# One load of all edge data in the head of a graph layer, in place of loads inside its loop

## The reference

```python
C = 0.5 * (cos(edge_length * (PI / 10)) + 1.0) * ((edge_length <= 10) & (edge_length >= 0))
h = gelu(edge_attr @ f_w0 + f_b0)          # 20000 x 50 -> 128
h = gelu(h @ f_w1 + f_b1)
h = gelu(h @ f_w2 + f_b2)
h = gelu(h @ f_w3 + f_b3)
msg = (x @ lin1_w)[src] * (h * C[:, None])
agg = segment_sum(msg, dst, num_segments=1250)     # dst is sorted
out = gelu(agg @ lin2_w + lin2_b) @ lin_w + lin_b
return layernorm(x + out)
```

## Time and profile before

| what | value |
|---|---|
| median of three runs | 312.98 us (311.64 to 314.6) |
| profiled execution | 311.7 us, its span 309.9 us |
| PE matmul busy | 249.1 us, 80% |
| PE weight loads | 161.5 us, 52% |
| POOL busy | 156.9 us, 51% |
| ACT busy | 113.4 us, 37% |
| DVE busy | 103.4 us, 33% |
| mean granted clock of PE | 0.775 of 2.4 GHz |
| DMA | 14,483 packets, 17.54 MB |

### The profile page before, as it was taken

The page is one execution under the profiler, slowest core; times in us unless marked ns, Lnnn a source line. Parts: engine busy times, 40 slices in busy tenths (PEclk is TensorE's granted clock), DMA queues, the critical chain, the costliest instruction groups (busy, mean ns, idle before and its releaser), DMA issues.

```text
span 309.9 us, 3660 instructions
## 1 busy us (share of the span) xinstructions
PE 249.1 (80%) x990; PEld 161.5 (52%) x990; DVE 103.4 (33%) x218; ACT 113.4 (37%) x181; POOL 156.9 (51%) x168
## 2 busy tenths in 40 slices
PE   3697939966995997699399869939984994998990
PEld 3344625735663473566257456625743662665760
DVE  5612430514154051414324141432414052335015
ACT  2544412433353243335224433522442352355033
POOL 7671747374555737455473755546474645630000
PEclk9899985796598579659957965995696599569768
DMA  6530211122112212211221221121122202210002
GB/s 206 154 103 20 68 53 52 27 78 59 42 40 65 68 26 77 60 43 32 66 65 26 77 67 44 34 64 57 34 77 54 57 21 73 64 31 0 0 0 83
DMA packets 14483, 17.54 MB, mean 57 GB/s; under 512 B 6512, under 2 KB 11533, under 8 KB 14478
## 3 DMA queue, kind: packets, MB, share of 16 engines
q0 software_dynamic: 5120, 10.50, 12.9%
q1 hardware_dynamic: 8632, 6.39, 7.2%
q10 hardware_dynamic: 726, 0.59, 0.7%
HBM read 16.19 MB, written 1.28 MB: 56 GB/s over the span
## 4 chain that ended last, share of the span: by engine, by line
PE 67%; another core or an unknown queue 15%; issue 7%; DVE 6%; DMA 2%; DVEq 1%; ACT 1%; SPq 0%; ACTq 0%
PE ps_even L430 9%; PE ps_even L406 9%; PE ps_agg_even L443 8%; PE ps_even L421 8%; PE ps_odd L421 8%; PE ps_agg_odd L443 7%; PE ps_odd L430 7%; PE ps_even L416 3%; PE ps_odd L416 3%; DVE messages L606 2%; DMA tables<-in_edge_tables 2%; DVE pre L591 1%; PE ps_even L507 1%; PE ps_odd L497 1%
## 5 line engine op out<-in xcount | busy, mean ns | idle before, releaser
L272 POOL DMA_INDIRECT gathered<-xf_dram,src_idx x152 | 146.9, 967 | 113.8 <-DVE messages L606 65.6
L443 PE MATMUL ps_agg_even<-onehot,messages 125*128 125x64 f32 x160 | 29.4, 346 | 41.4 <-DVE messages L606 33.9
L319 ACT ACTIVATE h<-ps_even,biases_sb 128x500 f32<-128x500 f32 x61 | 41.1, 674 | 57.7 <-PE ps_even L421 36.4
L443 PEld LDWEIGHTS ps_agg_even<-onehot,messages 125*128 125x128 f32 x160 | 28.1, 259 | 52.8 <-issue 44.1
L319 ACT ACTIVATE h<-ps_odd,biases_sb 128x500 f32<-128x500 f32 x61 | 41.1, 674 | 37.0 <-PE ps_odd L421 26.6
L317 ACT ACTIVATE h<-pre 125x512 f32<-125x512 f32 x40 | 25.2, 630 | 74.3 <-DVE pre L591 56.5
L591 DVE TENSOR_TENSOR pre<-ps_even,row_b_sb 125x512 f32<-125x512 f32 x20 | 13.8, 692 | 86.7 <-issue 55.9
L430 PEld LDWEIGHTS ps_even<-w_mlp_sb,h 128*125 128x125 f32 x160 | 26.4, 249 | 21.3 <-issue 19.1
L443 PEld LDWEIGHTS ps_agg_odd<-onehot,messages 125*128 125x128 f32 x160 | 29.8, 263 | 13.1 <-issue 13.1
L406 PE MATMUL ps_odd<-edge_in,w_mlp_sb 50*128 50x500 f32 x42 | 31.8, 848 | 0.0
L406 PE MATMUL ps_even<-edge_in,w_mlp_sb 50*128 50x500 f32 x42 | 31.6, 841 | 0.2 <-issue 0.2
(11 more groups left out here) (99 smaller groups left out, 159.1 us busy)
## 6 DMA issues: line engine op xcount, KB each, us to landing
edge_in<-in_edge_attrT SPq DMA_DIRECT2D x42, 97.7 KB
gathered<-xf_dram,src_idx POOLq DMA_INDIRECT x152
xf_dram<-xf_sb SPq DMA_DIRECT2D x2, 256.0 KB
lin_xT_sb<-in_lin_xT SPq DMA_DIRECT2D x1, 369.0 KB
src_idx<-in_srcT SPq DMA_DIRECT2D x22, 4.0 KB
lin_xT_sb<-in_lin_xT SPq DMA_DIRECT2D x1, 320.0 KB, 3.5
w_mlp_sb<-in_w_mlp ACTq DMA_DIRECT2D x1, 256.0 KB
out<-normed SPq DMA_DIRECT2D x1, 256.0 KB
```

The costliest lines, as they stand in the source:

```text
L272: nc.gpsimd.indirect_dma_start(out=gathered[:, b, t, :], out_offset=None, in_=xf_dram[:, :], in_offset=bass.IndirectOffsetOnAxis(ap=src_id ...
L319: nc.scalar.activation(out_ap, in_ap, GELU, bias=biases_sb[:, layer:layer + 1]).then_inc(done, 1)
L443: last = nc.tensor.matmul(ps_agg[b][:, 0:WINDOW], messages[:, slot, t, :], onehot[:, p % 2, b * TILES_PER_GROUP + t, :], start=(t == 0), s ...
```

## The change

All edge attributes and all gather indices are brought into SBUF before the loop. edge_in grows from two pairs to all twenty (40,000 bytes a partition), src_idx from 2 x 8 to 160 columns. The input array is laid out anew: one row for each of 114 partitions (50 for the even groups, 14 of zeros, 50 for the odd ones), so that one DMA loads both groups of one or several pairs. Six such DMAs cover the pairs 0, 1, 2-3, 4-7, 8-13 and 14-19; the first two are issued by SP behind the tables, the other four by ACT behind the weights. One DMA of 80 KB brings the indices. SP has nothing to do in the loop. PE's and POOL's pairs 2 to 19 are written out in place of the nine turns; ACT and DVE keep their loops.

```diff
+EDGE_CUTS = ((0, 1), (1, 2), (2, 4), (4, 8), (8, 14), (14, PAIRS))
-        src_idx = sb("src_idx", [ROWS, 2, PAIR_TILES], int32)
-        edge_in = sb("edge_in", [ODD_BASE + EDGE_FEAT, 2, GROUP])
+        src_idx = sb("src_idx", [ROWS, TILES], int32)
+        edge_in = sb("edge_in", [ODD_BASE + EDGE_FEAT, PAIRS, GROUP])
@@ block.sync
-            load_src(0, 0)
+            def load_edges(k):
+                p0, p1 = EDGE_CUTS[k]
+                sp.dma_start(edge_in[:, p0:p1, :], edge_attrT[:, p0:p1, :]).then_inc(edge_loaded[k], 16)
+            sp.dma_start(src_idx[:, :], srcT).then_inc(src_loaded, 16)
             ...
-            load_edges(0, 0)
-            load_src(1, 1)
+            load_edges(0)
+            load_edges(1)
             ...
-            with sp.Fori(0, passes) as r:
-                ...
-            sp.sem_inc(loads_drained, 1)
@@ block.gpsimd
-                with pool.Fori(0, TURNS - 1) as j:
-                    ...
+                for g in range(RAW_GROUPS, GROUPS):
+                    b = g % GATHER_SLOTS
+                    pool.wait_ge(message_done, r * GROUPS + g + 1)
+                    pool.sem_inc(group_begun, 1)
+                    for t in range(TILES_PER_GROUP):
+                        tile = g * TILES_PER_GROUP + t
+                        nc.gpsimd.indirect_dma_start(
+                            out=gathered[:, b, t, :], out_offset=None, in_=xf_dram[:, :],
+                            in_offset=bass.IndirectOffsetOnAxis(ap=src_idx[:, tile:tile + 1], axis=0),
+                        ).then_inc(gather_landed[b], 16)
@@ block.scalar, behind the loads of w_mlp, biases and row_b3
+            for k in range(2, len(EDGE_CUTS)):
+                p0, p1 = EDGE_CUTS[k]
+                act.dma_start(edge_in[:, p0:p1, :], edge_attrT[:, p0:p1, :]).then_inc(edge_loaded[k], 16)
@@ block.tensor
-                with pe.Fori(0, TURNS - 1) as j:
-                    before = r * TURNS + j
-                    for p in (2, 3):
-                        ...
+                for p in range(2, PAIRS):
+                    layer2(first, p)
+                    scatter(first, p - 1, 0)
+                    layer3(first, p, 0)
+                    scatter(first, p - 1, 1)
+                    layer3(first, p, 1)
+                    for k in range(3, len(EDGE_CUTS)):
+                        if EDGE_CUTS[k][0] == p + 1:
+                            pe.wait_ge(edge_loaded[k], 16)
+                    layer1((p + 1) % PAIRS)
+                    layer4(first, p)
```

More of the change, by code:

```diff
@@ L135, in gnn_layer @@
         tables_loaded = sem("tables_loaded")
-        src_loaded = [sem(f"src_loaded_{q}") for q in range(2)]
+        src_loaded = sem("src_loaded")
         w_loaded = sem("w_loaded")
         late_loaded = sem("late_loaded")
-        edge_loaded = [sem(f"edge_loaded_{s}") for s in range(2)]
-        loads_drained = sem("loads_drained")
+        edge_loaded = [sem(f"edge_loaded_{k}") for k in range(len(EDGE_CUTS))]
         raw_landed = [sem(f"raw_landed_{g}") for g in range(RAW_GROUPS)]
@@ L265, in _ @@
                         out=raw_x[:, g, t, :], out_offset=None, in_=x_nodes[:, :],
-                        in_offset=bass.IndirectOffsetOnAxis(ap=src_idx[:, 0, tile:tile + 1], axis=0),
+                        in_offset=bass.IndirectOffsetOnAxis(ap=src_idx[:, tile:tile + 1], axis=0),
                     ).then_inc(raw_landed[g], 16)
[L269 to L275, removed]
             pool.wait_ge(passes_ready, 1)
@@ L280, in _ @@
             with pool.Fori(0, passes) as r:
-                pool.wait_ge(src_loaded[1], r * (16 * TURNS) + 16)
-                for b in (2, 3):
-                    pool.wait_ge(message_done, r * GROUPS + b + 1)
+                for g in range(RAW_GROUPS, GROUPS):
+                    b = g % GATHER_SLOTS
+                    pool.wait_ge(message_done, r * GROUPS + g + 1)
                     pool.sem_inc(group_begun, 1)
-                    gather(b)
-                with pool.Fori(0, TURNS - 1) as j:
[L287 to L294, removed]
+                    for t in range(TILES_PER_GROUP):
+                        tile = g * TILES_PER_GROUP + t
+                        nc.gpsimd.indirect_dma_start(
+                            out=gathered[:, b, t, :], out_offset=None, in_=xf_dram[:, :],
+                            in_offset=bass.IndirectOffsetOnAxis(ap=src_idx[:, tile:tile + 1], axis=0),
+                        ).then_inc(gather_landed[b], 16)
         @block.scalar
@@ L400, in _, with layer1 @@
             pe.wait_ge(w_loaded, 48)
-            def layer1(loads, slot):
-                pe.wait_ge(edge_loaded[slot], loads)
+            def layer1(pair):
                 for b in range(2):
                     rows = slice(b * ODD_BASE, b * ODD_BASE + EDGE_FEAT)
-                    nc.tensor.matmul(ps1[b][:, 0:GROUP], w0[b], edge_in[rows, slot, :],
+                    nc.tensor.matmul(ps1[b][:, 0:GROUP], w0[b], edge_in[rows, pair, :],
                                      start=True, stop=True).then_inc(l1_done, 1)
-            layer1(32, 0)
+            pe.wait_ge(edge_loaded[0], 16)
+            layer1(0)
             pe.wait_ge(passes_ready, 1)
@@ L466, in _ @@
                 layer3(first, 0, 1)
-                next_layer1(first, 0)
+                pe.wait_ge(edge_loaded[1], 16)
+                layer1(1)
                 layer4(first, 0)
@@ L475, in _ @@
                 layer3(first, 1, 1)
-                next_layer1(first, 1)
+                pe.wait_ge(edge_loaded[2], 16)
+                layer1(2)
                 layer4(first, 1)
```

54 lines of the change are left out of this document (5 added, 49 removed).

## The result

The change makes the kernel slower: 339.35 us (median of four, 333.49 to 343.07) against 312.31 (311.58 to 314.6) for the kernel before beside it. The ratio is 1.070, 95% interval [1.058, 1.082]. A slower state of the chip lengthens some executions of every kernel (here two of four, the profiled one of 343.07 us, span 341.2, among them), so ratios, and every "A against B" from here on, are taken between the mean times of the others, here 334.6 against 312.7. These 7% are 22 us. The forecast was 319 with 315 to 326 as its own range: the sign is right, the size is missed by more than a factor of three.

The account below looks back on a forecast made before the run. Hold and clock, not arithmetic or gathers, were taken to set the loop's pace. The late store's 6.4 us plus 0 for the loop, added to the median 312.98, gave 319.4, said as 319; own range 315 to 326, whole range 280 to 328.

Parts of the forecast that it names:

- Loop loads, back edge and written-out code: SP's loop loads, PE's back edge, PE's and POOL's written-out pairs: gain or cost 0, straight code at most 5 us.
- The hold: In head and loop: PE's layer 4 results exist, but the signal freeing their reader, VectorE's bias sum, comes 5 us late.
- The large loads lie on six engines: Head: edge loads of 114 rows use six of 16 DMA engines, 34.5 us of work, full until about 40 us.
- The queues take turns by packet: Head: store packets alternate with ACT's large ones, so the xf_dram stores finish at 36 to 41 us, taken as 38.
- 0 for the loop: Loop's term in the sum: the change neither gains nor costs time there, 0 us.
- The change leaves both alone, so the loop keeps its pace: Loop: gathers and fast short matmuls, taken as the hold's condition, stay, so the pace doesn't change.
- Pairs 2 and 3 need nothing more: Loop start: no further delay after pair 1, as POOL takes 10 us a pair against a pace of 13.7.
- the gathers with fast short matmuls: Head and loop: the hold comes when gathers run while PE does short matmuls at the full clock.
- the 6.4: Head: with gathers begun at 38 us, pair 1's messages come at 49.8 in place of 43.4, 6.4 us later.
- Rival 1: Loop: the hold hangs on SP's loads or the back edge and goes; 258 us, or 288 by half; chance 0.28.
- Rival 2: Head: stores get through early, by byte-wise turns or 16 engines; 313 us, or down to 309; chance 0.20.
- Rival 3: Head: raw_x gathers or PE's code arrive late through six crowded engines; 323 to 333 us; chance 0.10.

Follow-up runs that it names:

- e3: Kernel before with only PE's and POOL's turns written out, SP's loads still in the loop, on a chip without holds: 239.19 us, before 237.47.
- e12: The kernel of e3 on a chip with the holds: 313.21 us, kernel before 311.65.
- e11: The kernel of e6 on a chip with the holds: 313.47 us, kernel before 311.65, ratio 1.011.
- e10: Kernel before without its 152 gathers of xf_dram, messages computed from ones, on a chip with the holds: 209.77 us, against 306.0.
- e4: Kernel before plus ACT's four large loads in the head, into a tile nobody reads, on a chip without holds: 261.47 us, before 237.47.
- e6: Changed kernel, 114 rows, with SP issuing the four large loads after the xf_dram stores landed, on a chip without holds: 238.86 us, before 239.34.
- e9: Changed kernel with 128 rows, large loads behind the stores, eight gather slots for four, VectorE's loop written out, chip with holds: 319.62 us, before 312.3.
- e8: Changed kernel with four spare columns behind each pair, so large loads go in 2,000-byte packets, chip with holds: 334.58 us, before 312.3, ratio 1.084.
- e1: Changed kernel with edge tile and source padded from 114 to 128 rows, on a chip without holds: 245.53 us, before 237.47.

## Why the prediction was wrong

Right were these steps, each with what bears it out. Loop loads, back edge and written-out code are worth nothing that these times show (e3, e12, and e11 with all three gone). The hold needs the gathers: the head of the changed kernel has none while POOL waits, and e10 has none at all; the forecast had this from three places of one trace. The large loads lie on six engines: six of sixteen are 37.5%, and the two queues show 37.9% in 24 to 36 us. The queues take turns by packet. The store is therefore late, pair 1 is late with it, and the order of two issues is the whole loss (e4 makes it on a chip of the second kind; e6 there and e11 on the first kind remove it).

The step that failed is "0 for the loop", with the sentences behind it, "The change leaves both alone, so the loop keeps its pace" and "Pairs 2 and 3 need nothing more: POOL takes 10 us for a pair and the pace is 13.7". It took POOL's idle 113.8 us for slack and the hold for something of a fixed length. But a POOL that starts late finds free slots and runs 24 gathers in a row, and the hold beside them is longer: PE's layer 4 of pair 2 ends at 63.2 us and its sum comes at 77.2, 14.0 us late, where the sums of the kernel before were 4 to 5 late beside bursts of eight. Pair 2's messages are 21.0 us late, and pair 1's second ones had been 10.7. e9 bears this out: its first burst is of 24 gathers too, and VectorE has PE's result of 28.3 us only at 46.1, 17.8 late; beside the 23 of e11 it was 9.6. Why a signal is held longer beside a longer burst isn't shown.

From the first gather to the last it takes 258.6 us before, 254.2 after, and 248 to 262 in e8, e9, e11 and e12, with starts between 14.2 and 43.4. This looks like a phase with a length of its own, so that a later start is paid in full; I don't take it as shown, since pair 1's messages follow the first gather by 6.3 us in the changed kernel and by 27 to 48 in the others. That a store done by 31.6 us would have cost nothing was tested on no chip with the holds. On the other chips the start is paid by a plainer cause, POOL back to back: 192 to 197 us from first to last in e1 to e6.

What pointed at the failed step was in front of me. The earlier trace rows has the held sum at 70.77, and the last gather of its burst, at 68.05 in the same timeline, ends at 69.0. I looked at what starts near the hold (SP's issue, a back edge) and made "the gathers with fast short matmuls" its condition, but never set the hold beside the burst or asked what a longer burst would do to it.

A term of the sum was mis-sized too, the 6.4. The store was priced at 38 us and took until 42.5, and the first messages of pair 1 came when forecast by luck: the 11.8 us from block to messages was read where the gathers had long landed and was used where the gathers themselves were the last to come. The first four give messages 6.3 us after the first gather, the second four 11.3, so the odd group of pair 1 was 10.7 us late. With 6.4 replaced by 10.7 the forecast would have said 324; the other 11 us are about what the lengthened hold adds. A slip without effect on the sum: ACT's rows are of 4,000 bytes too (pairs 2 and 3), and not of 8,000 and 12,000 alone.

Of the forecast's signs the DMA share near 6/16 and pair 1's messages near 50 us came, the latter by that luck. The first gather was due near 38 and came at 43.4. Waits of 4 to 5 us before ps_odd's sum once a turn did not come: the 19 waits of over 2 us on "remote" run from 2.1 to 18.8, eleven of them before other sums.

Rival 1 had the better eye for one thing, that the holds may be worth more than their sum in the chain: where there are none the kernel takes 232 to 244 us, and rival 1 had worked out 258 with a store at 38. But the change doesn't remove their condition. Rival 2's time is what happens with the stores ahead (e6, e11). Rival 3's raw gathers held nobody, but the edges of pair 0 were late, by 5 us in place of 2, hidden in the wait for the store.

Open is what makes the chips differ. The same kernel takes 304 to 322 us on some and 232 to 244 on others, with the holds as the visible difference, and no experiment here could switch them on or off on one chip other than by taking the gathers away. Each chip was used at one time only, so chip and time aren't separated. Which queue or engine keeps PE's signal back while POOL gathers isn't shown either; the profile says only "remote".

## What to carry to other kernels

Before an engine's idle time is taken for slack, set its bursts beside the waits of the others: if the waits lie at its bursts turn after turn, the engine may be part of what sets the pace, however idle it looks, and what a late start does to its bursts has to be priced; a version without its work (e10) tests this. A large load is better issued once the small store that others wait for has landed (here SP issued it then, in place of ACT): the two queues swapped packet for packet on each engine, and 512 bytes then cost as much time as the 12,000 beside them. Loads ahead of the loop didn't pay here, where the loop's loads were hidden: the version without the fault can't be told from the kernel before (1.011 [0.972, 1.050]).

## What the runs showed of the hardware

- One kernel, two paces: 304 to 322 us on two chips and 232 to 244 on two others, in the same code.
- PE's signals reached their readers late while gathers ran, on chips of the first kind: 4 to 5 us beside the bursts of eight of the kernel before, 2 to 7 beside those of the changed kernel, 14.0 beside its burst of 24, 17.8 beside e9's. In the kernel before the wait ended 0.3 to 1.8 us after the burst at ten of ten places. In the changed kernel 12 of 19 such waits end between 0.4 us before and 4.1 after a burst's end; of the others two end 1.1 and 1.2 us before the end of a burst of eight, and five 1.6 to 11.9 us before the end of bursts of 15 or 16. In e11 it is 9 of 19. So the end of a burst doesn't always release the signal.
- An issue can stall its engine for long: 6.5 us for one of SP's stores behind the bulk (9.2 in e1), and 19 us for ACT's four large loads when their packets are of 2,000 bytes (then 10.8 for its next one), against 0.4 us for an ordinary one.
- Two queues on one engine swap after every row. The DMA view of the changed kernel in 26.05 to 26.52 us:
```profile
q10 hardware_dynamic: 6, 0.07, 35.8%
q1 hardware_dynamic: 6, 0.00, 2.2%
```
  Six engines carry one row of 12,000 bytes and one of 512 each in 0.47 us. The Trainium skill (DMA: Bandwidth & Descriptors, section Queues, rings and completion order) has an engine switch between queues at packet boundaries and drain a packet, typically 9 to 17 descriptors, from one ring before it does. The trace disagrees on the length of a turn, which is one row here, and the measurement decides.
- Six DMA engines alone moved 26 KB per us each (1.81 and 0.08 MB in 12 us, over six), sixteen together 25 (e1, 397 GB/s in 14 to 22 us).
